# Preparing the first delta round's decay factors, inputs and gate weights in the joining phase

## What is computed

```python
q = silu(conv(x @ Wq)); k = silu(conv(x @ Wk)) * D ** -0.5; v = silu(conv(x @ Wv))   # causal, 4 taps
alpha = sigmoid(x @ Wa + ba); beta = sigmoid(x @ Wb + bb)
def step(St, inp):
    q_, k_, v_, a_, b_ = inp
    sk = einsum('bhij,bhj->bhi', St, k_)
    err = sk - v_
    Sn = a_ * St - b_ * err[..., None] * k_[..., None, :]
    return Sn, einsum('bhij,bhj->bhi', Sn, q_)
o = layernorm(o) * ln_w + ln_b
out = (o * sigmoid(x @ Wg)) @ Wo
```

## Time and profile before

| | us |
|---|---|
| median of 3 runs (2934.01 to 2935.45) | 2934.44 |
| the profiled execution | 2929.95 |
| its span | 2928.1 |
| joining phase in it | 983 to 1128 |
| delta phase in it, from | 1128 |
| PE busy | 2786.4 (95%) |
| DVE busy | 1760.7 (60%) |
| ACT busy | 1216.3 (42%) |
| POOL busy | 608.1 (21%) |

### The profile page before, as it was taken

How to read it: one execution, slowest core, us unless ns; L and a number is a source line. 1 busy time by engine, 2 the same in 40 slices (tenths; PEclk the granted TensorE clock), 3 DMA queues, 4 the chain that set the end, 5 groups by cost and what they waited for, 6 DMA issues and landing times. The chain is left out here.

```text
span 2928.1 us, 37502 instructions
## 1 busy us (share of the span) xinstructions
PE 2786.4 (95%) x13038; PEld 1565.3 (53%) x13039; DVE 1760.7 (60%) x4357; ACT 1216.3 (42%) x2247; POOL 608.1 (21%) x669
## 2 busy tenths in 40 slices
PE   6999989999999987999999999999999999999787
PEld 3444434445555444666666666666666666554232
DVE  5767762011111374777877778877778777438586
ACT  3555431111222245455555555545565445422232
POOL 2112100401111312133113332133331233200000
PEclk9999989999999998999999999999999999999899
DMA  3101123022112652011110011100211002245113
GB/s 130 49 1 44 43 109 163 29 85 95 64 64 64 235 190 91 16 45 66 66 44 30 30 69 62 44 30 30 73 66 37 33 27 74 88 142 203 58 47 101
DMA packets 78420, 215.20 MB, mean 73 GB/s; under 512 B 12064, under 2 KB 12976, under 8 KB 69680
## 3 DMA queue, kind: packets, MB, share of 16 engines
q1 hardware_dynamic: 57472, 165.79, 15.6%
q0 software_dynamic: 9264, 28.36, 3.0%
q10 hardware_dynamic: 11520, 18.92, 1.8%
HBM read 156.25 MB, written 56.79 MB: 73 GB/s over the span
## 5 line engine op out<-in xcount | busy, mean ns | idle before, releaser
L2326 DVE SCALAR_TENSOR_TENSOR c_conv<-c_ps_pj,c_conv_t,c_conv 128x511 f32<-128x511 f32 (+2 forms) x450 | 336.0, 747 | 29.8 <-ACT c_conv L2148 19.2
L1813 POOL TENSOR_SCALAR c_gate<-c_gate 128x512 f32<-128x512 f32 x64 | 37.9, 619 | 991.7 <-DVE c_block_L L2359 991.7
L1890 PE MATMUL c_ps_pj<-c_xs,c_w_v 128*128 128x512 f32 x480 | 225.8, 593 | 0.0
L1890 PE MATMUL c_ps_pj<-c_xs,c_w_q 128*128 128x512 f32 x360 | 177.0, 614 | 0.0
L1911 PE MATMUL c_ps_pj<-c_w_g,c_xs 128*128 128x512 f32 x384 | 172.7, 592 | 0.0
L1890 PE MATMUL c_ps_pj<-c_xs,c_w_k 128*128 128x512 f32 x360 | 166.5, 599 | 6.1 <-DMA c_xs<-xt_d 6.1
L2148 ACT ACTIVATE c_conv<-c_ps_pj,c_conv_t 128x512 f32<-128x512 f32 x150 | 116.4, 776 | 54.0 <-PE c_ps_pj L1890 25.6
L1203 DVE TENSOR_TENSOR x_act<-x_hs,x_ps_u 128x352 f32<-128x352 f32 x40 | 20.9, 522 | 191.5 <-ACT x_hs L1188 191.5
L2211 ACT ACTIVATE c_err<-c_negL 32x128 f32<-32x128 f32 x256 | 78.6, 307 | 134.0 <-DVE c_negL L2392 129.3
L2356 DVE TENSOR_TENSOR c_block_X<-c_block_X,c_block_t 128x58 f32<-128x58 f32 (+6 forms) x448 | 117.7, 263 | 15.4
L2353 DVE TENSOR_TENSOR c_block_t<-c_block_L,c_block_X 128x58 f32<-128x58 f32 (+6 forms) x448 | 117.6, 262 | 14.9
(11 more groups left out here) (523 smaller groups left out, 5969.0 us busy)
## 6 DMA issues: line engine op xcount, KB each, us to landing
c_G<-cum_d SPq DMA_DIRECT2D x16, 1024.0 KB, 4.8
c_xs<-xt_d SPq DMA_DIRECT2D x16, 1024.0 KB, 4.8
ot_d<-c_oT ACTq DMA_DIRECT2D x64, 256.0 KB, 2.0
b_w_gu<-in_w_gu SPq DMA_DIRECT2D x8, 1408.0 KB, 20.7
y_slots<-x_y SPq DMA_DIRECT2D x40, 256.0 KB, 2.0
a_x<-in_x SPq DMA_DIRECT2D x8, 1024.0 KB, 6.6
d_x<-x SPq DMA_DIRECT2D x32, 256.0 KB, 2.9
d_switch<-in_switch_w SPq DMA_DIRECT2D x4, 2048.0 KB, 17.2
```

What stands on the lines that cost most here:

```text
L1890: mm = e.matmul(bank_of[xb][u][:, :], w["kqv"[u // HG]][:, k, (u % HG) * DH:(u % HG + 1) * DH], xs[xb][:, k, :], start=(k == 0), stop=(k = ...
L2326: e.scalar_tensor_tensor(oc, bank_of[buf][u][:, 0:SEQ - s], conv_t[buf][:, m, h, TAPS - 1 - s:TAPS - s], oc, ALU.mult, ALU.add).then_inc(c ...
```

## The change

1. In the joining phase, round 0's share of the tables (4 blocks, 4 heads: 16 columns) is made early. For batch 0 DVE adds the bias after `x_shift(1)` (`z0_done`), ACT makes its soft-plus after `take_turned(1)`, DVE forms the logs in batch 2 after `sums(2)`, PE makes one product `cum0` ahead of `turn(2)` and its transpose ahead of `gate_logits(2)`, ACT copies both (`cum0`, `row0`), DVE makes the gain of round 0, SP stores `row0` as `cum0_d` and loads it to all partitions of G; POOL adds mask and gain.
2. SP also loads, in the joining phase, the taps for round 1, `w_g`, xs[0] and xs[1]. The loads at the start of the delta phase are gone, but for `ln_w` and `ln_b`.
3. G, `not_yet` and xs[1] become tiles that both phases hold; two of the four `picked` tiles of the joining phase lie in G and xs[1].
4. At the end of the joining phase `unit(11)` goes ahead of the cumulative products, `tap(11)` ahead of their copy, `silu(7)` to the other first silus; one change of table is gone, and the silus of the four v heads move to round 0 of the delta phase, after `next_tap(2)`.

```diff
+        picked = [[tab["G"]..., tab["xs1"]], [sb(f"picked1{k}", [P, TPB, DM]) for k in range(2)]]
+        cum0, row0 = soft[:, TPB, 0:TPB * HG], soft[0:TPB * HG, NT - TPB:, :]...
...
 SP, loop over b
+                if b == 0:
+                    e.dma_start(first.conv_t[1][:, :, :, :], io["conv_t"][0]).then_inc(delta_loaded, 16)
+                if b == 1:
+                    e.wait_ge(down_ready, len(downs))
+                    e.dma_start(first.w["g"][:, :, :], io["w_g"][0]).then_inc(delta_loaded, 16)
+                    e.wait_ge(xt_stored, 16 * 2)
+                    e.dma_start(first.xs0[:, :, :], io["xt_d"][0]).then_inc(delta_loaded, 16)
+                if b == 2:
+                    e.wait_ge(row0_copied, 1)
+                    e.dma_start(io["cum0_d"], row0).then_inc(row0_stored, 16)
+                    e.wait_ge(y_done, TPB * 3)
+                    e.wait_ge(row0_stored, 16)
+                    e.dma_start(tab["G"]..., io["cum0_d"]...partition_broadcast(P)).then_inc(G0_loaded, 16)
+                    e.dma_start(tab["xs1"][:, :, :], io["xt_d"][1]).then_inc(delta_loaded, 16)
...
 POOL
+            e.wait_ge(G0_loaded, 16)
+            e.wait_ge(gain0_done, 1)
+            for c in range(TPB):
+                e.tensor_tensor(G[:, c], G[:, c], tab["not_yet"]..., ALU.add).then_inc(G0_masked, 1)
+                e.wait_ge(G0_masked, c + 1)
+                e.tensor_tensor(G[:, c], G[:, c], tab["gain"][:, 0, 0, c, :]..., ALU.add).then_inc(G0_biased, 1)
...
 PE, loop over b
+                if b == 2:
+                    e.wait_ge(middle_made, 1)
+                    e.wait_ge(logs0_done, 2)
+                    e.matmul(cum_ps[0][:, 0:TPB * HG], from_middle[:, :], log_decay[:, 0, 0, :, :]...).then_inc(cum0_ready, 1)
                 turn(b)
...
+                if b == 2:
+                    e.wait_ge(cum0_copied, 1)
+                    e.transpose(cum_ps[2][0:TPB * HG, 0:P], cum0, con["ident"][:, :]).then_inc(row0_ready, 1)
                 gate_logits(b)
-            e.wait_ge(middle_made, 1)
+            unit(UNITS - 1)
+            e.wait_ge(row0_copied, 1)
             e.wait_ge(logs_done, NG)
             for dst, mask in zip(cum_ps, (from_middle, con["before"], con["upto"], con["ones"])):
...
-            unit(UNITS - 1)
...
 ACT
+                if b == 2:
+                    e.wait_ge(cum0_ready, 1)
+                    e.activation(cum0, cum_ps[0][:, 0:TPB * HG], ACT.Copy).then_inc(cum0_copied, 1)
                 take_turned(b)
+                if b == 1:
+                    soft_plus(slice(0, TPB), z0_done, soft0_step)
+                if b == 2:
+                    e.wait_ge(row0_ready, 1)
+                    e.activation(row0, cum_ps[2][0:TPB * HG, 0:P], ACT.Copy).then_inc(row0_copied, 1)
...
-            for u in range(2 * HG - 1):
+            for u in range(2 * HG):
                 silu(u)
...
+            tap(UNITS - 1)
...
-            tap(UNITS - 1)
-            e.preload_act_table_set("silu_and_others")
-            for u in range(2 * HG - 1, UNITS):
-                silu(u)
...
 DVE
+                if b == 2:
+                    e.wait_ge(soft0_step, 3)
+                    for i, table in enumerate((log_decay, log_beta)):
+                        e.scalar_tensor_tensor(table[:, 0, 0, :, :], z[...], 0.0, soft[...], ALU.min, ALU.subtract).then_inc(logs0_done, 1)
...
                 if b == 1:
+                    e.wait_ge(ab_loaded, 32)
+                    e.wait_ge(z_ready, 1)
+                    e.tensor_tensor(z[:, 0:TPB, :], z_ps[:, 0:TPB, :], bias..., ALU.add).then_inc(z0_done, 1)
                     taps(1)
                 taps(3 * b - 1)
+                if b == 2:
+                    e.wait_ge(cum0_copied, 1)
+                    e.tensor_tensor(tab["gain"][:, 0, 0, :, :]..., log_beta..., cum0, ALU.subtract).then_inc(gain0_done, 1)
...
+            e.wait_ge(G0_biased, TPB)
             e.tensor_tensor(flat(tab["gain"]), flat(log_beta), ..., ALU.subtract).then_inc(tables_done, 1)
-            taps(UNITS - 1)
...
 delta phase, SP
-            load_cum(0)
-            load_round(1)
-            load_w("g", 0)
-            e.dma_start(xs[0][:, :, :], io["xt_d"][0]).then_inc(xs_loaded[0], 16)
...
 delta phase, POOL
-            e.tensor_scalar(not_yet[:, :], con["upto"][:, :], -1.0, 1e30, ALU.add, ALU.mult).then_inc(cleared, 1)
-            bias_gains(0)
...
 delta phase, ACT
+                else:
+                    for h in range(HG):
+                        e.activation(vT_first[:, h, :], vT_first[:, h, :], ACT.Silu).then_inc(v_first_done, 1)
```

More of the change, by code:

```diff
@@ L1261, in phase_moe_out @@
         cum, cum_rows = (yn[:, i, 0:2 * P].rearrange("p (k m) -> p k m", m=P) for i in range(2))
+        cum0, row0 = soft[:, TPB, 0:TPB * HG], soft[0:TPB * HG, NT - TPB:, :].rearrange("q j m -> q (j m)")
         turned = [pr.ps(st, f"o_ps_tp{i}", [P, KD, P]) for i in range(2)]
@@ L1384, in _ @@
                     unit(3 * b + 1)
+                if b == 2:
+                    e.wait_ge(middle_made, 1)
+                    e.wait_ge(logs0_done, 2)
+                    e.matmul(cum_ps[0][:, 0:TPB * HG], from_middle[:, :], log_decay[:, 0, 0, :, :].rearrange("p c h -> p (c h)"),
+                             start=True, stop=True).then_inc(cum0_ready, 1)
                 turn(b)
@@ L1451, in take_down, with soft_plus @@
                 e.dma_start(rows(io["y_shared"], b)[:, c, :], first.conv[:, i % STAGES, :]).then_inc(down_stored[i % STAGES], 16)
+            def soft_plus(of, done, step):
+                e.wait_ge(done, 1)
+                e.activation(soft[:, of, :], z[:, of, :], ACT.Abs).then_inc(step, 1)
+                e.wait_ge(step, 1)
+                e.activation(soft[:, of, :], soft[:, of, :], ACT.Exp, scale=-1.0).then_inc(step, 1)
+                e.wait_ge(step, 2)
+                e.activation(soft[:, of, :], soft[:, of, :], ACT.Ln, bias=1.0).then_inc(step, 1)
             e.preload_act_table_set("natural_log_exp_and_others")
@@ L1592, in gate_tables @@
 def gate_tables(pr, stack):
-    return {k: pr.sb(stack, k + "_all", [P, NG, NB, TPB, HG]) for k in
-            ("gain", "decay_before", "decay_upto", "decay_all")}
+    tab = {k: pr.sb(stack, k + "_all", [P, NG, NB, TPB, HG]) for k in
+           ("gain", "decay_before", "decay_upto", "decay_all")}
+    tab["not_yet"] = pr.sb(stack, "c_not_yet", [P, P])
+    tab["G"] = pr.sb(stack, "c_G", [P, TPB, HG, P])
+    tab["xs1"] = pr.sb(stack, "c_xs1", [P, KD, SEQ])
+    return tab
 def phase_delta(pr, con, XT, tab, given):
@@ L1981, in a_round @@
                 e.wait_ge(silu_done, CONVS * r + CONVS + 4)
+                if not after_first(r):
+                    e.wait_ge(v_first_done, HG)
                 for c in range(TPB):
```

57 lines of the change are left out of this document (39 added, 18 removed).

## The result

| | before | after |
|---|---|---|
| median of five runs each, on one chip | 2934.60 us (2934.01 to 2937.72) | 2919.39 us (2916.86 to 2921.06) |
| ratio | | 0.9945, 95% interval 0.9930 to 0.9959 |
| profiled execution (its span) | 2929.95 us (2928.1) | 2917.18 us (2915.4) |

The two profiled executions differ by 12.8 us.

The account below looks back on a forecast made before the run. The seam between the phases was taken as bound by chains of waits, everything after 1145 by PE alone. 8.2 + 5.2 - 3.0 = 10.4 us gave a median of 2924.1 us, with 2921.0 to 2928.0 as the 8-in-10 range.

Parts of the forecast that it names:

- Part 1: Delta phase start: with xs and G already there, the second block's products start at 8.0 us, 8.2 us earlier.
- The rival with the unit at the lower clock: Delta phase's first unit runs at the lower clock: gain 8.3 or 7.0 us, 2926.1 to 2927.4; 14%.
- Part 2: Joining phase loop: small steps added to a full chain make it 3.0 us later; bounds 1.3 and 4.5.
- (a): Batch 1 of the loop: DVE waits for the first logits and adds the bias before taps(1), +0.8 us.
- (b): Batch 2 of the loop: two logs of 16 columns, +0.3 us.
- (c): Loop: the copy of cum0 before take_turned(2), +0.2 us.
- (d): Loop: ACT waits to copy row0 with tap 6 behind it; taps(6) starts at 1089.4 instead of 1086.37.
- The rule weighed: Shared-port lock: a DVE addition could wait a whole POOL step, 1.2 us, 4.9 in all; rows showed cost, not full block.
- Part 3: End of the joining phase: last take_turned to delta phase takes 17.5 us instead of 22.7, gaining 5.2 us.
- the rival at 2922.4: End of joining phase: PE's cumulative products run at the full clock after less idle time, 1.7 us more gain; 10%.
- The layout and the cover of G: G done by 1107, wanted at 1122, costs nothing; rival: new SBUF places lengthen all 16 rounds, 2940 us, 3%.
- the rival of a lost joining phase: Loop loses 4.5 us and the end gives 3.5, so only the delta phase's gain stays: 2926.5 to 2927.5; 12%.

Follow-up runs that it names:

- The pair of experiments with one chain each: Kernel before with the new end plus early w_g, xs and conv_t: ratio 0.9982; changed kernel without those early loads, G still early: 0.9976.
- the order taken back: Changed kernel with unit 11, the last tap, silu 7 and the v silus back where they stood before: ratio 0.9983.
- the shifts: Two or four more matmuls ahead of the first round's first gate product: kernel before 2926.52 and 2931.31 us, changed kernel 2911.89 and 2911.87 us.
- The two steps: Changed kernel with ACT's row0 copy moved behind tap 6 and POOL starting on G after DVE's last x offset: ratios 0.9947 and 0.9938.
- early inputs and end: Kernel before with the new end, new tile places and early w_g, xs and conv_t, G loaded and biased as before: ratio 0.9982.

## Why the forecast was right in kind and short in size

- **What bounds the seam.** Right: chains of waits, two of them at the delta start. The pair of experiments with one chain each shows it best.
- **Part 1, 8.2 us.** Measured 8.6 (16.0 less 7.41). The products and transposes took 3.65 us instead of 4.5, since the first ones stood 0.22 us apart, at the full clock, before the distance rose to 0.43; the unit took 3.76 instead of 3.45. The v silus cost nothing, as costed. The rival with the unit at the lower clock is refuted, by two kernels (3.92 and 3.60 us).
- **Part 2, 3.0 us.** Measured 3.2 to 3.3, right by errors that cancel. (a) taps(1) +0.8: DVE's addition at 1053.15 and the taps at 1053.36 make it 0.82 more against `o_y_nb` than before. (b) and (c), 0.5: 0.15. (d), 1.7 (3.0 less 1.3): 1.1, as PE was ready sooner. Not in the sum: 1.2 for POOL beside DVE. I had looked for the four additions of the residual as the nearest operation, and passed over the offset of x, an operation of 0.15 us with two operands on chip and the whole batch behind it.
- **The rule weighed.** It was the trace that I read too weakly. The Trainium skill, page "SBUF — State Buffer", section "SBUF: two separate sides", says that the loser blocks for the whole instruction. Here DVE's 0.15 us became 1.05 us and ended with POOL's step, 1104.92 and 1104.90. The trace agrees, but for the 0.13 us by which 0.15 us of work begun at 1104.90 would have ended later. The price wasn't 4.9 us, since only one operation met a step at a bad moment.
- **Part 3, 5.2 us.** Measured 6.7: **the term that was missized**. Up to the products the working holds (ACT's soft-plus ends 9.6 us after the tap, products at 10.7 against 10.55). From their start to the end of the last exponential I took 4.35 us; it took 2.6. Unit 11 now stands straight ahead of the products, so they ran at the full clock (1.72 us behind the unit, 3.25 with the order taken back). That was the rival at 2922.4 with 10%, which I tied to the idle time ahead of the products. I had changed PE's order there myself and kept the old price.
- **The seam's sum, 10.4 us.** Measured 12.1. From the median that makes 2922.3, within the range.
- **The step that failed.** The prediction says that what comes after 1145 is bound by PE alone, so that "whatever brings PE's work of 1144.57 forward brings the rest forward by as much". PE's work behind the seam was put down as only shifted, with no term of its own. It came 12.1 us forward at the seam and 17.2 us at the end: E gave 1.3 and F 3.7 us. PE's order is the same there, but two pieces of it that come after a wait for something else took other times: the last round's first unit 5.40 us instead of 6.65, and the eight matmuls behind F's first wait 3.60 instead of 5.30. For E the shifts show that this goes with where the wait falls; for F only the place is shown, and the reason stays open.
- **How the number left the range.** With the seam as measured the forecast would be 2922.3, inside; with E and F it is 2917.3, outside. The measured 2919.39 lies 2.1 us above that, which differences between executions account for: the changed kernel's profiled one had the standstill (+6.7) and an earlier start of the joining phase (-2.1), and the median lay 2.2 us above it, not the 4.5 that I held constant (-2.3).
- **The layout and the cover of G**: right. G's bias ended at 1108.37 and was asked for at 1127.45.
- **Slips in the working**, without weight: the rival of a lost joining phase comes to 2926.2 to 2927.2 us by its own terms, not 2926.5 to 2927.5, and the steps under (d) add up to 89.6, not 89.4.

No kernel that was run is measurably faster than the changed one. The two steps are 2.2 us better in the loop, but with them the out phase takes 2.6 us more, and no total shows a gain.

## What to carry to other kernels

Where two chains end at the same wait, cost them together: one alone gave 0, the other 3.1, both 8.4 us. When an order is changed, price each matmul by what PE does ahead of it in the new order, not by its old row. A gain of a few us far up a program is worth that plus or minus what PE's later waits make of it (here 5 us, a third of the result, and 1.6 us with both kernels shifted by 1.72 us). So compare sections of like traces, and shift the work by one or two us on purpose before such a difference is credited to a change.

## What of the hardware was not expected

- What PE loses to the lower clock behind a wait isn't fixed by the length of the wait. Behind 3.2 to 3.5 us the same eight passes took 5.4 us or 6.5 to 6.8 us in all 18 traces (3.60 at the full clock), and a shift by 1.72 us turned the one into the other in both kernels; behind 2.25 us eight passes took 3.60 us or 5.30.
- The same program repeats its value, though its executions reach the place up to 9.5 us apart: 5.40 us in three traces of the changed kernel, 6.65 to 6.72 us in three of the kernel before.
- 3.43 us of more work on PE made the kernel before only 0.1 to 0.3 us longer, by its traces from A's start to the end.
- ACT stood still with a finished block before it, in five of 18 traces, four of them on one chip: 8 us in the changed kernel's first, 10 us with early inputs and end. The DMA engines were as busy in traces without it. No record names what it waited for.
- The load of G (1024 KB, one row spread to all partitions) took 7.3 us from issue to landing at the start of the delta phase with four other loads issued behind it, 7.0 us with none behind it, and 4.6 us in the joining phase. Taking the other loads away gained little.
